# A four-layer graph network in one kernel: ids two groups ahead in the sort, q gathered before k and v, clears on GpSimd, the next round's state inside the main loops, counts as columns

## The reference

```python
# layer 0: sum of the edge features at dst, then an MLP 256 -> 512 -> 128
agg = segment_sum(edge_attr, dst);  x = ln(x + relu([agg, x] @ W1 + b1) @ W2 + b2)
# layer 1: attention with 8 heads of 16; the softmax runs over ALL edges (axis 0)
Q, K, V = x @ WQ + bQ, x @ WK + bK, x @ WV + bV
score = clip(sum(Q[dst] * K[src]) / 4, -5, 5);  attn = softmax(score, axis=0)
h = segment_sum(attn * V[src], dst) @ WO + bO      # then ln, feed-forward, ln, residual, ln
# layer 2: an MLP on each edge, whose sum at dst enters a node MLP
e = relu([x[src], x[dst]] @ We1 + be1) @ We2 + be2
x = ln(x + x + relu([x, segment_sum(e, dst)] @ Wn1 + bn1) @ Wn2 + bn2)
# layer 3: degree-normalised sum over the edges of a row (row = src), then a linear map
dis = where(deg > 0, rsqrt(deg), 0)
x = ln(x + segment_sum(dis[row] * dis[col] * x[col], row) @ W.T + b)
```

## Time and profile before

| | us |
|---|---|
| runs | 5488.76, 5492.09, 5493.91 |
| the profiled execution | 5486.88 |
| its span | 5485.0 |
| PE busy in the span | 5016.6 (91%) |
| DVE | 4408.0 (80%) |
| ACT | 3289.6 (60%) |
| POOL | 1958.7 (36%) |
| landing of a list's load in layer 2 after its issue (median of 98) | 5.5 |

### The profile page before, as it was taken

One profiled execution on the slowest core, in us unless ns is written; L12 is line 12 of the kernel. 1 busy time (PEld: TensorE's weight loads), 2 busy tenths in 40 slices (PEclk: granted clock), 3 DMA queues, 4 the chain that ended last, 5 costly groups with the idle time before them and its releaser, 6 DMA issues. The chain is left out here.

```text
span 5485.0 us, 164969 instructions
## 1 busy us (share of the span) xinstructions
PE 5016.6 (91%) x56178; PEld 4464.3 (81%) x56254; DVE 4408.0 (80%) x7721; ACT 3289.6 (60%) x5897; POOL 1958.7 (36%) x1946
## 2 busy tenths in 40 slices
PE   5888888799999999999997869999999997899996
PEld 4777777699999999999997759999999996656555
DVE  8999992277777777777776659999999996588886
ACT  3444443377777777777774437777777773466651
POOL 3433345533333333333332445555555552300000
PEclk9999999899999999999998979999999998899988
DMA  4443431222222222222221123333333331000000
GB/s 161 155 147 147 153 138 55 77 99 93 90 96 91 93 90 97 90 94 93 90 98 46 40 75 128 133 129 132 127 132 127 130 129 33 0 1 0 0 0 24
DMA packets 175998, 498.05 MB, mean 91 GB/s; under 512 B 24861, under 2 KB 61728, under 8 KB 169500
## 3 DMA queue, kind: packets, MB, share of 16 engines
q1 hardware_dynamic: 169528, 491.34, 25.3%
q10 hardware_dynamic: 6372, 5.43, 0.3%
HBM read 466.39 MB, written 30.33 MB: 91 GB/s over the span
## 5 line engine op out<-in xcount | busy, mean ns | idle before, releaser
L1555 PE MATMUL ps<-kv_table,stage 128*128 128x256 bf16 x7203 | 1180.0, 273 | 29.7 <-ACT stage L1461 29.5
L1864 POOL TENSOR_TENSOR parts<-rest 128x512 bf16<-128x512 f32 x588 | 654.0, 1118 | 613.3 <-DVE rest L1923 607.0
L2062 PE MATMUL ps<-a_table,stage 128*128 128x128 bf16 x7203 | 794.6, 219 | 41.2 <-DVE stage L1899 41.2
L2065 PE MATMUL ps<-window,stage 128*128 128x128 bf16 x7350 | 812.1, 219 | 0.0
L1558 PE MATMUL ps<-window,stage 128*128 128x128 bf16 x7350 | 810.8, 219 | 0.0
L1519 POOL TENSOR_TENSOR message<-message 128x512 f32<-128x512 f32 (+1 forms) x441 | 445.5, 1010 | 899.1 <-ACT message L1468 899.1
L1387 DVE TENSOR_TENSOR product<-ps,q_kept 128x512 f32<-128x512 f32 (+1 forms) x637 | 426.3, 669 | 376.0 <-ACT message L1447 303.2
L1445 ACT ACTIVATE q_kept<-ps 128x512 f32<-128x512 f32 (+1 forms) x637 | 369.7, 580 | 544.8 <-PE ps L1558 536.6
L1555 PEld LDWEIGHTS ps<-kv_table,stage 128*128 128x128 bf16 x7203 | 629.5, 98 | 69.2 <-issue 30.3
L1558 PEld LDWEIGHTS ps<-window,stage 128*128 128x128 bf16 x7350 | 616.9, 98 | 55.9
L1981 ACT ACTIVATE parts<-ps 128x512 bf16<-128x512 f32 x588 | 349.1, 594 | 335.9 <-PE ps L2065 335.3
(11 more groups left out here) (368 smaller groups left out, 10876.9 us busy)
## 6 DMA issues: line engine op xcount, KB each, us to landing
stage<-lists SPq DMA_DIRECT2D x294, 768.0 KB, 4.0
edges<-in_edge_attr SPq DMA_DIRECT2D x49, 2240.0 KB, 8.3
stage<-lists SPq DMA_DIRECT2D x98, 896.0 KB, 5.5
window<-qkv_rows SPq DMA_DIRECT2D x49, 288.0 KB, 5.4
window<-ab_rows SPq DMA_DIRECT2D x49, 192.0 KB, 5.0
qkv_rows<-kv_table SPq DMA_DIRECT2D x21, 384.0 KB, 2.5
qkv_rows<-q_parts SPq DMA_DIRECT2D x21, 192.0 KB, 2.0
ab_rows<-a_table SPq DMA_DIRECT2D x21, 192.0 KB, 2.0
```

What stands on the lines that cost most here:

```text
L1555: nc.tensor.matmul(kv_ps[n % 2][:, i, :], from_src, kv_table[:, tile, q, :], start=(q == 0), stop=(q == 2))
L1864: pool.tensor_tensor(parts_of(n)[:, 0:nt, D:2 * D], rest[BUFFER[n]][:, 0:nt, :], middle[BUFFER[n]][:, 0:nt, :], ALU.subtract).then_inc(low ...
L2062: nc.tensor.matmul(to[:, i, :], from_src, a_table[:, tile, q, :], start=(q == 0), stop=False)
L2065: last = nc.tensor.matmul(to[:, i, :], own, window[d][:, (3 + q) * D:(4 + q) * D], start=False, stop=(q == 2))
```

## The change

- `ids_rows` and `ids` are stored field by field, (4, E) in place of (E, 4), so each id field of a window lies in one piece: 35 elements or 70 bytes per partition and field.
- In the start-up the weights are loaded from ACT's queue behind its conversions, and POOL clears `acc` behind the first two of the fields.
- `id_step` is called two groups ahead and stands behind the bucket one-hot of the next group.
- Attention gathers the q of a batch's four tiles first; a new semaphore `queried1` lets ACT copy q, `gathered1` now releases the copy of v.
- The clears of `acc` at the start of layers 1 to 3 are replaced by POOL copies of a column of zeros in the node stages before, one per lane and step, in front of the lane's `split_rows`.
- The re-sort is cut in two. `resort_ahead_dve` and `resort_ahead_sp` step the state and load the first ids inside the main loop (behind group 0, in layer 3 behind four one-hots). `resort_dve` starts with the ids there; the payload is made by POOL in `resort_pool`; SP loads once more ahead at the end of each pass.
- `counts` becomes (128, 49, 2), holding a column of in-degrees and one of self loops per group; the matmul L2088 and the add L1931 go. In layer2_nodes DVE makes `bias_of` = be2 times the count of a node (one product per 128 columns), and PE adds it by a product with the identity, 128 columns each.
- `sum0`, `sum1a` and their like become one semaphore `residual`; `x_kept` goes.

```diff
-            edge_ids = words(hot_words[1], 0, 2 * CE, BF16).rearrange("p (n w) -> p n w", w=4)
+            edge_ids = words(hot_words[1], 0, 2 * CE, BF16).rearrange("p (w n) -> p w n", w=4)
...
-                            sp.dma_start(ids[:, ds(g, 1), :, :].rearrange("p s c w -> p (s c w)"),
-                                         ids_rows[ds(at, SG), :].rearrange("(p c) w -> p (c w)", c=GC)
+                            sp.dma_start(ids[:, ds(g, 1), :, :].rearrange("p s w c -> p (s w) c"),
+                                         ids_rows[:, ds(at, SG)].rearrange("w (p c) -> p w c", c=GC)
...
-                        inside_dve(dve, inside[:, :], owned[:, :], numbers[:, :, 0], g).then_inc(selected, 1)
+                        inside_dve(dve, inside[:, :], owned[:, :], numbers[:, 0, :], g).then_inc(selected, 1)
                         dve.wait_ge(selected, j * 2 + 2)
-                        dve.tensor_tensor(bucket[b][:, :], numbers[:, :, 3], inside[:, :], ALU.mult)
-                        dve.tensor_tensor(target[b][:, :], numbers[:, :, 1], inside[:, :], ALU.mult).then_inc(split_ids, 1)
+                        dve.tensor_tensor(bucket[b][:, :], numbers[:, 3, :], inside[:, :], ALU.mult)
+                        dve.tensor_tensor(target[b][:, :], numbers[:, 1, :], inside[:, :], ALU.mult).then_inc(split_ids, 1)
...
-                    def rank_step(j, g, b, load=None):
-                        if load is not None:
-                            id_step(j + 1, g + 1, 1 - b, load)
+                    def rank_step(j, g, b, load=None, ahead=True):
                         dve.wait_ge(prefixed, j + 2)
                         pick_dve(dve, chosen, bucket_hot[b]).then_inc(picked, 1)
                         dve.wait_ge(picked, j + 1)
                         ranks_dve(dve, chosen, rank_all[:, ds(g, 1), :].rearrange("p s c -> p (s c)")).then_inc(ranked, 1)
+                        if ahead:
+                            bucket_step(j + 1, 1 - b)
                         if load is not None:
-                            bucket_step(j + 1, 1 - b)
+                            id_step(j + 2, g + 2, b, load)
                         dve.wait_ge(ranked, j + 2)
                         dve.wait_ge(coded, j + 2)
                         rank_hot_dve(dve, rank_hot, rank_all[:, ds(g, 1), :].rearrange("p s c -> p (s c)"),
                                      rank_by4[:, :, :]).then_inc(rank_spread, 1)
-                        if load is not None:
...
                         id_step(first, 0, 0, first)
+                        id_step(first + 1, 1, 1, first)
...
+        def resort_load(sp, g, came):
+
+            at = first_edge(mybir.EngineType.SP, g)
+            sp.dma_start(again_ids[:, :, :], ids_rows[:, ds(at, SG)].rearrange("w (p c) -> p w c", c=GC)).then_inc(came, 16)
...
+        def resort_ahead_sp(sp, came, state, first):
 
             sp.wait_ge(state, first * 10 + 10 * NG)
             sp.sem_inc(sp_waited, 1)
+            resort_load(sp, 0, came)
...
+                sp.wait_ge(step, s * RESORT + 13 + 1)
                 sp.sem_inc(sp_waited, 1)
-                sp.dma_start(r["ids"].rearrange("p c w -> p (c w)"),
-                             ids_rows[ds(at, SG), :].rearrange("(p c) w -> p (c w)", c=GC)).then_inc(came, 16)
+                resort_load(sp, g + 1, came)
...
+            sp.wait_ge(came, first * 32 + total * 16 + 16)
+            sp.sem_inc(sp_waited, 1)
+            sp.sem_inc(came, (NG - 1) * 16)
...
-                rank_hot_dve(dve, r["rank_hot"], r["rank_now"], r["by4"]).then_inc(step, 1)
-                pay_with(dve, r["pay"], r["hot"], [r["ids"][:, :, 1 + w] for w in range(2)]).then_inc(step, 1)
-                after(13)
...
+        def resort_pool(pool, r, step, layer, first, total):
+
+            with pool.Fori(0, total) as g:
+                s = first + g
+                pool.wait_ge(step, s * RESORT + 4 + 1)
+                pool.sem_inc(pool_waited, 1)
+                pay_with(pool, r["pay"], r["hot"], [r["ids"][:, 1 + w, :] for w in range(2)]).then_inc(repaid[layer], 1)
+                pool.wait_ge(step, s * RESORT + RESORT + 1)
+                pool.sem_inc(pool_waited, 1)
...
+                            pool.wait_ge(hidden_ps0, (c + 1) * MB)
+                            pool.sem_inc(pool_waited, 1)
+                            pool.tensor_copy(acc[:, columns(n, l)], zero[:, :].broadcast_to([P, width(l)])).then_inc(acc_cleared, 1)
...
-                        act.wait_ge(gathered1, s + GATHERED + 1)
+                        act.wait_ge(queried1, s + 1)
                         act.wait_ge(product1, s + 1)
                         act.activation(q_kept[n % 2][:, 0:nt, :], q_ps[n % 2][:, 0:nt, :], ACT.Copy)
+                        act.wait_ge(gathered1, s + GATHERED + 1)
                         act.wait_ge(scattered1, s + 1 if n >= 2 else s + 2)
...
-                            own, from_src = hots[u % 2][0][:, at:at + P], hots[u % 2][1][:, at:at + P]
-                            for q in range(3):
-                                if tile == SELF:
-                                    nc.tensor.matmul(kv_ps[n % 2][:, i, :], own,
-                                                     window[d][:, (3 + 2 * q) * D:(5 + 2 * q) * D],
-                                                     start=(q == 0), stop=(q == 2))
-                                else:
-                                    nc.tensor.matmul(kv_ps[n % 2][:, i, :], from_src, kv_table[:, tile, q, :],
-                                                     start=(q == 0), stop=(q == 2))
+                            own, _ = hots_of(tile)
                             for q in range(3):
                                 last = nc.tensor.matmul(q_ps[n % 2][:, i, :], own, window[d][:, q * D:(q + 1) * D],
                                                         start=(q == 0), stop=(q == 2))
+                        last.then_inc(queried1, 1)
+                        for i, tile in enumerate(batch_tiles(b)):
+                            own, from_src = hots_of(tile)
+                            for q in range(3):
+                                if tile == SELF:
+                                    last = nc.tensor.matmul(kv_ps[n % 2][:, i, :], own,
+                                                            window[d][:, (3 + 2 * q) * D:(5 + 2 * q) * D],
+                                                            start=(q == 0), stop=(q == 2))
+                                else:
+                                    last = nc.tensor.matmul(kv_ps[n % 2][:, i, :], from_src, kv_table[:, tile, q, :],
+                                                            start=(q == 0), stop=(q == 2))
                         last.then_inc(gathered1, 1)
...
-                    dve.memset(acc[:, :], 0.0).then_inc(added2, 1)
-                    dve.memset(counts[:, :], 0.0).then_inc(added2, 1)
+                    dve.wait_ge(acc_cleared, 2 * NORMS)
...
                         dve.wait_ge(added2, j + ready)
-                        dve.tensor_tensor(self_dis[:, ds(g, 1)], self_dis[:, ds(g, 1)],
-                                          group_sum[d][:, 2 * D + 1:DIRECT], ALU.add)
-                        dve.tensor_tensor(counts[:, ds(g * P, P)], counts[:, ds(g * P, P)], GROUP_COUNTS, ALU.add)
+                        own_counts = counts[:, ds(g, 1), :].rearrange("p s w -> p (s w)")
+                        dve.tensor_tensor(own_counts, own_counts, group_sum[d][:, 2 * D:DIRECT], ALU.add)
                         dve.tensor_tensor(acc[:, ds(g * P, P)], acc[:, ds(g * P, P)], GROUP_ACC, ALU.add).then_inc(added2, 1)
...
+                        resort_ahead_dve(dve, state2, first)
...
                         for at in (0, DIRECT, D):
-                            nc.tensor.matmul(GROUP_ACC, group_sum[d][:, at:at + D], ident, start=(at == 0), stop=(at == D))
-                        nc.tensor.matmul(GROUP_COUNTS, group_sum[d][:, 2 * D:2 * D + 1], ident, start=True, stop=True
-                                         ).then_inc(group_ps2, 1)
+                            last = nc.tensor.matmul(GROUP_ACC, group_sum[d][:, at:at + D], ident,
+                                                    start=(at == 0), stop=(at == D))
+                        last.then_inc(group_ps2, 1)
...
                             pe.wait_ge(y_scaled, n * TURN + blocks_before(l - ROUND + 1) + TURN)
                             nc.tensor.matmul(half(l, 0)[:, 0:width(l)], we2_sb[:, :], acc[:, columns(n, l)],
-                                             start=True, stop=False)
-                            nc.tensor.matmul(half(l, 0)[:, 0:width(l)], be2_sb[:, :], counts[:, columns(n, l)],
-                                             start=False, stop=True).then_inc(agg_ps2, 1)
+                                             start=True, stop=False, skip_group_check=True)
+                            pe.wait_ge(biased2, n * TURN + blocks_before(l + 1) + TURN)
```

(13 more changed lines are left out.)

252 lines of the change are left out of this document (142 added, 110 removed).

## The result

The changed kernel takes 5279.98 us (median of 4 runs, 5275.35 to 5283.64) against 5491.2 for the kernel before, a ratio of 0.9615 with a 95% interval of 0.9598 to 0.9631: 211 us less. The forecast was 5350, 141 us less (142 in the span). The profiled execution has a span of 5281.8, 203.2 less than before, and this is where they went. The marks between stages are first and last matmuls of a kind, the same in both traces. Layer 1's edges go from the first to the last gather of k and v; after the change q's gather stands 1.2 us ahead of the first one, so that with the first gather of any kind as the mark layer 0's nodes give -1.7 and layer 1's edges -59.5.

The account below looks back on a forecast made before the run. PE was taken to bound the loops, so gains were its idle time plus PE work that disappears, and the seams between stages. Terms summed to -142.5 us: 5344.4 from 5486.88, forecast 5350 with the runs' median 5.2 above; range 5305 to 5410.

Parts of the forecast that it names:

- Layer 1's edges: Layer 1's edge loop: q matmuls first let ACT copy q sooner, taking three quarters of PE's 39.8 us of waits: -30.
- Start-up: Before the first ids: contiguous writes, acc cleared later, a shorter SP line: -6.5 us, ends -10 and -1.
- Sort: Sort loop: the moved id step no longer stands behind POOL's payload; PE's wait of 1.44 us goes in 49 groups: -70.
- A: Sort: half the gain, as rank_hot behind the id step becomes late, and payload and codes with it; +35 us, chance 0.10.
- C: Sort: at its new place the id step still meets POOL; +70 us, 5420, chance 0.06.
- D: Sort: an ids load's 512 short runs fall on one or two DMA engines, ahead of the edges; 5685 us, chance 0.03.
- Rival B: Layer 1's edges: no gain, the message is held by ACT's one-hots, not the copies' order; +30 us, 5380, chance 0.10.
- Re-sorts: Three re-sorts: state stepped earlier -6.5, payload to POOL -3.8, awaited second ids load +0.3 us each: -30 in all.
- Layer 1's nodes: Layer 1's node stage: POOL's clears add +1.1 us in the last step and 1 for contention.
- The start of layer 2's edges: Start of layer 2's edge stage: two DVE clears of 5.29 us go, the lists' DMA then decides: -3.1 us.
- Layer 2's edges: Layer 2's edge loop: a DVE add and PE matmul go per group, some of it turning into waits: -8 us.
- Layer 2's nodes: Layer 2's node stage: new bias products +0.8 us in each of 7 steps, degree chain +1, POOL's tail +1.1: +7.6.

Follow-up runs that it names:

- 74.6 alone: The kernel before with only the id step moved two groups ahead, ids in their old layout: 5415.2 us, 74.6 less (0.9867).

## Why the prediction was wrong, by its steps

The time lies 25 us below the range first of all because of layer 1's edges, where the forecast counted only PE's waits; the gain that it left out there, 28 us, is larger than the whole miss of the range. The clock in the node stages is the second step that it had wrong.

- **Start-up**, -6.5: -7.1. The three strided writes fell from 3.75 to 1.84, as forecast. The first product of the chain starts at 16.15 in place of 17.75. That is two things at once: the constants had landed by 8.9 in place of 15.85, and POOL's clear met DVE's first instructions, one of which took 5.6 us, the mishap that the near end of the range named and the sum left out. It cost little, since ACT's three conversions run to 14.4 beside it. For all this the sum took 1 us (its terms add up to 6.7, not 6.5), and 1.6 was measured; that it came so near is luck, two things left out that nearly cancel.

```profile
9.15 5.59 DVE L559 CAST ident_b<-cst 128x128 bf16<-128x128 f32 x1
...
16.15 1.84 DVE L576 SCALAR_TENSOR_TENSOR dst_hot<-dst_hot,pay 128x1624 bf16<-128x1624 bf16 x1
...
51.84 0.26 DVE L286 SCALAR_TENSOR_TENSOR inside<-ids,cst,owned 128x35 bf16<-128x35 bf16 x1
```

- **Sort**, -70: -70.4 in the trace, 74.6 alone. Right, mechanism and size: the gain is PE's wait and not DVE's saving. DVE, busy for 549 of 640 us, now has room. Rivals A, C and D are false: PE's only waits left are for ACT's list, so the loads of 512 runs of 70 bytes land in time.
- **Layer 1's edges**, -30: -60.7. This step failed most. "The two edge loops can give back at most 39 and 16 us of idle PE plus what PE work disappears" took the time of busy PE for fixed. Two terms: the waits gave 34, not 30, as they fell to 6.0; and 28 (44 ns on average in each of 637 scatters) came from the first pass behind a wider matmul. That is PE time that the page counts as busy. The prediction has no word on which matmul a scatter stands behind. Rival B is false.
- **Re-sorts**, -30 in three: the sort itself, from the last add to the codes, gave 10 each time, as worked out. The seams behind, to the next product that both kernels have, gave back 3.5, nothing and 4.4 (3.52, 4.85 and 4.67 before, 7.01, 4.88 and 9.04 after). I had put 0.3 for an awaited load. Issuing it earlier brought nothing; 2.6 of the 3.5 and 2.8 of the 4.4 are the instruction that comes late, and the rest is not explained. In layer 1 that loss goes with attention's new wait, which the prediction priced at nothing.
- **Layer 1's nodes**, +2.1: POOL's tail, its work behind the last step, is +0.9 (forecast 1.1), but the steps are 10.4 shorter, 8.8 of it by the clock. The prediction looked at no single step: three of six took 30.8 us and one 32.6, of which 27.6 were work and 3.2 and 5.0 the low clock.
- **The start of layer 2's edges**, -3.1: -7.5 from the stage's first DVE instruction to ACT's first (12.69 before, 5.18 after), and another 1.9 between POOL's end and that DVE instruction. Two terms of the sum were mis-sized. I took 5.5 plus 1.5 for the list's landing from its issue, and it is there 4.3 after, though the window's load is issued 0.64 ahead of it: 2.7. And SP issues it 0.84 behind DVE's first instruction, where it was 2.57: 1.7, which I had put at nothing.

```profile
3090.45 1.02 SPq L1172 DMA_DIRECT2D stage<-lists  x2
```

```profile
3094.79 1.58 ACT L2035 ACTIVATE stage<-stage,lane 128x1536 bf16<-128x1536 int16 x1 [31.28 <-DMA stage<-lists]
```

- **Layer 2's edges**, -8: -3.8. PE's product went, and PE waits longer for DVE's slot_hot, 26.7 in place of 13.0, which takes back most of what it gained. The end of the range for "turns into waits" was nearer than my value:

```profile
PE ps L2124 <- DVE slot_hot L1962: 26.7, 48, 0.6
```

- **Layer 2's nodes**, +7.6: -10.2, of which 6.6 are the clock in three of the seven steps and 2.5 the first step. Where neither is in play a step is 0.2 shorter, not 0.8 longer, and that is the part that the change itself has in this stage. Before's second, third and sixth step, and after's third, with the granted clock at the end:

```profile
4647.83:4663.28 15.45, 15.12 (x84) 11.81 (x84) 7.38 (x24) 7.63 (x25) 7.73 (x16) 1.00 0.00 0
4663.28:4681.96 18.68, 18.34 (x84) 14.04 (x84) 7.39 (x24) 7.61 (x25) 7.73 (x16) 0.82 0.00 0
4712.90:4730.03 17.13, 16.80 (x84) 12.99 (x84) 7.43 (x24) 7.60 (x25) 7.73 (x16) 0.90 0.00 0
```

```profile
4481.30:4496.50 15.20, 13.89 (x90) 12.32 (x90) 9.03 (x31) 7.60 (x25) 9.11 (x20) 1.00 0.00 0
```

The wait for the first bias is real, 1.14 where I had 1.4 us of lateness. What failed is the price of the matmuls behind it: I kept the main products at 0.63 as in the rows, and they took 0.43.
- **Layer 3's edges**, -5.2: -5.6 for the start; the stage itself another -2.9, not explained.
- The range came from the same mistake: the far ends in the two edge loops were idle time of PE, and the clock had only a few us. Of the 61 us that the span gained beyond the sum, 31 are in layer 1's edges, some 18 are the clock in the two node stages (8.8, and 6.6 and 2.5), and the rest is spread over the starts of the stages. The clock's part is luck: nothing in the change aims at it.
